# Seven small SBUF buffers are declared earlier, and everything declared behind them starts 224 bytes higher

## The reference, cut to what matters

```python
mod = (_silu(L0_c) @ L0_wmod).reshape(8, 6, 1, -1)
sa, ca, ga, sb, cb, gb = ...                       # six rows of mod
ga, gb = (2 * (g >= 0) - 1) * jnp.maximum(jnp.abs(g), 0.25)   # for g in ga, gb
h = _layernorm(x) * (1 + ca) + sa
lhs, rhs = h * w_lhs, h * w_rhs
attn = softmax(einsum('nsd,ntd->nst', lhs, rhs), axis=2)
x = x + ga * einsum('nst,ntd->nsd', attn, h)
h = _layernorm(x) * (1 + cb) + sb
x = x + gb * (relu(h @ W1 + b1) @ W2 + b2)
```

## Time and profile before

| | |
|---|---|
| Time, median of 3 runs | 679.18 us (678.83 to 679.28) |
| The profiled execution | 679.18 us |
| Its span, first to last instruction | 677.4 us |
| PE busy | 672.5 us, 99% |
| PEld busy | 620.4 us, 92% |
| DVE busy | 545.9 us, 81% |
| ACT busy | 500.2 us, 74% |
| POOL busy | 295.2 us, 44% |
| DMA | 88.57 MB, mean 131 GB/s |

### The profile page before, as it was taken

The page is one execution under the profiler, slowest core; times in us unless marked ns, Lnnn a source line. Parts: engine busy times, 40 slices in busy tenths (PEclk is TensorE's granted clock), DMA queues, the critical chain, the costliest instruction groups (busy, mean ns, idle before and its releaser), DMA issues.

```text
span 677.4 us, 13532 instructions
## 1 busy us (share of the span) xinstructions
PE 672.5 (99%) x4551; PEld 620.4 (92%) x4551; DVE 545.9 (81%) x1139; ACT 500.2 (74%) x749; POOL 295.2 (44%) x311
## 2 busy tenths in 40 slices
PE   9999999999999999999999999999999999999998
PEld 8688889998999999999999989999899999999897
DVE  4798889887899879998799887988789987778321
ACT  2376787976889777895878949888688976747563
POOL 3551365225353345442645235542535334615544
PEclk9999999999999999999999999999999999999999
DMA  8131664237632377124671256513763246311210
GB/s 295 55 81 62 194 188 148 72 97 237 194 96 74 123 238 231 48 89 149 202 210 62 93 186 195 145 62 124 216 195 84 75 146 197 97 41 65 85 48 31
DMA packets 72897, 88.57 MB, mean 131 GB/s; under 512 B 6880, under 2 KB 64800, under 8 KB 72864
## 3 DMA queue, kind: packets, MB, share of 16 engines
q1 hardware_dynamic: 72864, 88.15, 41.6%
HBM read 51.66 MB, written 36.47 MB: 130 GB/s over the span
## 4 chain that ended last, share of the span: by engine, by line
PE 99%; DVE 0%; DMA 0%; issue 0%; SPq 0%
PE col L662 9%; PE col L661 9%; PE col L660 9%; PE acc L582 8%; PE acc L583 8%; PE acc L588 8%; PE score L766 8%; PE score L762 8%; PE score L763 8%; PE score L650 4%; PE score L651 4%; PE score L649 4%; PE score L755 4%; PE score L623 2%; PE score L551 1%; PE score L727 1%
## 5 line engine op out<-in xcount | busy, mean ns | idle before, releaser
L1249 POOL TENSOR_TENSOR hid_lo<-hid,hid_hi 128x512 fp32r<-128x512 f32 x127 | 175.9, 1387 | 258.3 <-ACT hid_hi L791 257.6
L787 ACT ACTIVATE hid<-col,b1T 128x512 f32<-128x512 f32 x128 | 87.1, 681 | 72.6 <-PE col L662 67.8
L582 PE MATMUL acc<-W2hi,hid_hi 128*128 128x256 f32 x480 | 118.0, 280 | 0.0
L583 PE MATMUL acc<-W2lo,hid_hi 128*128 128x256 f32 x480 | 116.6, 277 | 0.0
L762 PE MATMUL score<-V,Phi 128*128 128x258 f32 x448 | 108.7, 281 | 0.0
L763 PE MATMUL score<-V,Phi 128*128 128x256 f32 x448 | 108.5, 281 | 0.0
L662 PE MATMUL col<-h2hi,W1lo 128*128 128x512 f32 x256 | 101.0, 395 | 0.0
L660 PE MATMUL col<-h2hi,W1hi 128*128 128x512 f32 x256 | 100.7, 393 | 0.0
L661 PE MATMUL col<-h2lo,W1hi 128*128 128x512 f32 x256 | 100.7, 393 | 0.0
L791 ACT ACTIVATE hid_hi<-hid 128x512 fp32r<-128x512 f32 x128 | 81.0, 633 | 23.2 <-PE acc L588 15.6
L582 PEld LDWEIGHTS acc<-W2hi,hid_hi 128*128 128x128 f32 x480 | 90.3, 188 | 1.4
(11 more groups left out here) (168 smaller groups left out, 1476.5 us busy)
## 6 DMA issues: line engine op xcount, KB each, us to landing
block_rows<-blocks SPq DMA_DIRECT2D x29, 512.0 KB, 2.8
blocks<-block_rows SPq DMA_DIRECT2D x116, 128.0 KB, 2.9
x_cur<-x SPq DMA_DIRECT2D x16, 512.0 KB, 3.9
ln_t<-x SPq DMA_DIRECT2D x14, 512.0 KB, 4.8
score_blocks<-stage SPq DMA_DIRECT2D x14, 512.0 KB, 2.9
S<-score_blocks SPq DMA_DIRECT2D x56, 128.0 KB, 3.0
S<-quarter_blocks SPq DMA_DIRECT2D x56, 96.0 KB, 2.6
out<-x_mlp SPq DMA_DIRECT2D x8, 512.0 KB, 5.3
```

What stands on the lines that cost most here:

```text
L582: nc.tensor.matmul(o, hi, W2hi[:, it, :], start=(it == 0 and (apart or t % 2 == 0)), stop=False, skip_group_check=True)
L583: nc.tensor.matmul(o, hi, W2lo[:, it, :], start=False, stop=False, skip_group_check=True)
L787: nc.scalar.activation(hid[:, n % 2, :], col[n % 2][:], ACT.Relu, bias=b1T[:, n % FT:n % FT + 1]).then_inc(col_read, 1)
L1249: G.tensor_tensor(hid_lo[:, n % RING, :], hid[:, n % 2, :], hid_hi[:, n % RING, :].bitcast(F32), ALU.subtract).then_inc(hid_lo_done, 1)
```

## The change

Two lines of declarations move from the end of the list to a place behind wl and wr. No instruction, wait, shape or type is changed; PSUM and DRAM are as they were.

```diff
@@ -261,6 +261,9 @@
         W2hi, W2lo = sb("W2hi", [P, FT, D], F32R), sb("W2lo", [P, FT, D], F32R)
         b1T, b2T = sb("b1T", [P, FT]), sb("b2T", [P, DK])
         wl, wr = sb("wl", [P, DK]), sb("wr", [P, DK])
+
+        w_sign, w_abs, w_root = sb("w_sign", [P, 2, DK]), sb("w_abs", [P, 2, DK]), sb("w_root", [P, 2, DK])
+        root_power, root, root_r, sign_r = sb("root_power", [P, 2, DK]), sb("root", [P, DK]), sb("root_r", [P, DK]), sb("sign_r", [P, DK])
 
         mod_cols = sb("mod_cols", [P, NB, 4 * DK])
         mod_a, mod_b = sb("mod_a", [P, 2 * DK]), sb("mod_b", [P, 2 * DK])
@@ -315,9 +318,6 @@
         inv_sum = sb("inv_sum", [P, 1])
         nb1, nb2 = sb("nb1", [P, T]), sb("nb2", [P, T])
         mod_l, mod_r = sb("mod_l", [P, 2 * DK]), sb("mod_r", [P, 2 * DK])
-
-        w_sign, w_abs, w_root = sb("w_sign", [P, 2, DK]), sb("w_abs", [P, 2, DK]), sb("w_root", [P, 2, DK])
-        root_power, root, root_r, sign_r = sb("root_power", [P, 2, DK]), sb("root", [P, DK]), sb("root_r", [P, DK]), sb("sign_r", [P, DK])
```

## The result

The changed kernel takes 686.28 us (685.74 to 687.78, 4 runs) against 679.0 us for the kernel before beside it, ratio 1.011 with a 95% interval of 1.0094 to 1.0127. That is 7.3 us more, on the side and nearly at the size of the rival "G loses its free state" (686.9 us), and outside the stated range.

What follows compares the result with a forecast made beforehand. PE was taken to bound the kernel, as the sum of distances between matmul starts. Every term was taken as 0, so 679.18 + 0 = 679.2 us, with an 8 in 10 range of 675.3 to 685.2 us.

Steps and rivals of the forecast that it cites:

- G loses its free state: Slower rival: the shift breaks the address relation of hid to W2; 1536 matmuls x 5 ns, 7.7 us, 686.9 us; chance 0.13.
- What bounds the kernel: Whole kernel: PE busy 672.5 of 677.4 us and 99% of the chain, so time is the sum of matmul start distances.
- The buffers themselves, DVE, ACT, POOL, DMA: Seven moved buffers, other engines and transfers: each taken as 0; outer bounds 1.6 us for DVE, 2.9 us for DMA.
- AV: Matmuls on V and Phi: 0 taken, the shift only deals V's tile starts out anew; bounds plus and minus 1.3 us.
- SC: Matmuls on R and L: 0 taken, both operands move and their distance stays; bounds -3.7 and +3.0 us.
- F: Matmuls on h2 and W1: 0 taken though h2 moves and W1 stays; bounds -7.7 and +4.6 us.
- G: Matmuls streaming W2 and loading hid: 0 taken because W2's start stays, cannot gain; upper bound +7.7 us.
- surplus: Matmul time above the estimated free duration: 5 ns at 256 and 258 columns, 7 at 384, 10 at 512; together 18 us.
- The argument against the rival: Against the slower hid and W2 case: h2 and W1 also stand at 192 against 128, yet pay 10 ns per 512 columns.
- The chances: Whole kernel: no change 0.40, slower 0.34 (F and SC 0.21, G 0.13), faster 0.26.
- The rival's price: All of G slowed by AV's surplus: 1536 matmuls x 5 ns = 7.7 us, giving 686.9 us; chance 0.13.

Runs made afterwards that it cites:

- e3: Kernel before with 224 unused bytes ahead of everything, so all starts shift and all distances stay; 679.54 us, ratio 1.0004.
- e1: Changed kernel with an unused 32-byte buffer behind the seven moved ones, restoring every start modulo 256; 678.89 us, ratio to before 0.9998.
- m1: Kernel before with 224 unused bytes ahead of h2hi alone, putting h2 minus W1 at 32; 681.74 us, ratio 1.0042.
- e4: Kernel before with 32 unused bytes ahead of W2hi and 224 behind W2lo, so only W2 gets other starts; 685.64 us, ratio 1.0092.
- m2: Kernel before with 192 unused bytes ahead of h2hi alone, putting h2 minus W1 at 0; 681.30 us, ratio 1.0029.
- e2: Kernel before with 224 unused bytes ahead of hid_hi and 32 behind hid_lo, so only these two get other starts; 685.22 us, ratio 1.0091.
- b1: Kernel before with unused bytes: 64 ahead of Rhi, 192 ahead of hid_hi, 192 ahead of h2hi; 679.70 us, ratio 1.0014.
- b4: Kernel before with unused bytes: 64 ahead of Rhi and 192 ahead of hid_hi, none ahead of h2; 676.91 us, ratio 0.9965.

## Why the prediction was wrong, step by step

- *What bounds the kernel.* Right. PE is 99% of the chain before and after, and all of the cost is in distances between matmul starts.
- *The buffers themselves, DVE, ACT, POOL, DMA.* 0, right: e3 moves every buffer by the same 224 bytes and e1 moves the seven to their new place, and both stay within 0.1% of before.
- *AV.* 0, right (118.8 and 118.7 ns). The reason given, that the shift only deals the tiles out anew, is not what holds it: V and Phi move together, and in e3 every start changes and AV's sum does not. The tiles did not change places either: L763 is longest at tile 4 (284.9 ns) and shortest at tile 7 (277.0) before, and in the changed kernel again (284.8 and 277.3).
- *SC.* 0, right (-0.1 us), for the reason given beside it, that the distance between its two operands stays.
- *F.* 0 taken, +1.3 us measured, within the bound of +4.6. Alone, in m1, F's move costs F 1.8 us.
- *G, the step that failed.* "G is the only group without surplus and W2 the only moving float32r operand that starts at a multiple of 128, which does not change. So I take 0." It measures +6.0 us. W2's start was not what spared G: e3 puts W2 at 96 and G stays at 276 ns, e4 puts it at 160 and G pays. What spared it was the distance to hid, and that was what the change did alter for G. The upper bound of +7.7 us and its place were right; the value between the bounds was read from a coincidence of one buffer. "G alone has none" was read from L588 and from the median of L582: the means of L582 and L583 are 280 and 277 ns, and G's mean distance of 115.0 ns lies 1.7 above the 113.3 of a piece behind another piece. So G had something to lose and a little to gain, about 1536 x 1.7 = 2.6 us as an estimate.
- *The argument against the rival.* "F has 192 against 128 too, with the roles changed, and does pay" compared 512 columns with 256 and took one failure for a refutation. F has good and bad distances of its own, as the two kernels show that move h2 alone (229.0 ns at 0 in m2, 233.5 at 32 in m1), and they need not be G's.
- *The chances.* Two readings of G were open, start or distance, and no row of before told them apart, since in one layout both are fixed. A range that leaves out the full price of such a rival, 686.9, on a chance of 0.13 was too narrow.
- *The rival's price.* That 686.9 comes so near to 686.28 is in part luck. Its mechanism held, but G pays 6.0 us and not 7.7; F's 1.3 us, which the rival did not have, make up most of the rest.

The rule of the Trainium skill that was weighed, in "SBUF — State Buffer", section on who interferes with whom, gives PE two read ports, one for the moving operand and one for the weights, independent of each other. The runs do not bear it out as a rule for time: with the same instructions and widths, the distance between the two operands decides whether a matmul of G takes 115.0 ns (before) or 118.9 (e2) on average. The measurement decides. The rule of the Trainium skill that the gap of a single matmul depends on width alone ("TensorE: Matmul & The Clock Gate", section on the back-to-back issue gap) fails for this stream in the same place.

What stays open: why 64 is G's good distance, what in SBUF the two reads share, and how the two paces hold themselves. The runs show that the cost goes with the distance between the two operands modulo 256; a collision of the two reads would fit it, and was not shown. Open too is which two reads they are, those of one matmul or those that run at the same time.

## What to carry to other kernels

On a kernel that is bound by float32r matmuls, treat the order of SBUF declarations as part of the schedule: a buffer of a few bytes declared earlier is a change of every distance across it. Compare the time from start to start of a matmul group with that of its best twin of the same width; if they differ, try fillers between the streamed and the loaded operand before touching instructions. Check the whole kernel each time, since a better distance in one group can put the next one into its slow pace.

## What the runs showed of the hardware that was not expected

- The time of G's 256 column float32r matmuls, each with a weight load of its own, depends on the distance between the moving and the loaded operand in SBUF, modulo 256 bytes: 115.0 ns on average at 64, 118.9 and 119.1 at 32 with nothing else changed (e2, e4), 118.5 to 120.3 at 0, 96, 128 and 192 with other groups' distances changed too. A shift of both by 224 bytes costs nothing (e3, 679.54 us), nor does one of hid alone by 256 (e1, 678.89 us).
- At the good distance there are still two paces, 113 and 117.5 ns, and the group that ran before decides which. In b1, 34 of the 37 pieces of G that come behind F take 1.41 us or more, and all 29 behind AV about 1.38; in the kernel before, all 37 behind F stay under 1.40.
- The same holds for F at one and the same distance: behind AV it takes 233.3 ns in the kernel before and 229.2 in b4, where of the four groups only SC and AV have another distance.
- Starts of 16 or 48 bytes modulo 64 cost DVE and ACT nothing that shows: L1133 reads V's second half there and L868 writes it, with medians of 1216 and 1047 ns, against 1220 and 1047 for aligned buffers.
